# Graph layers on one Trainium2 core: one program per engine in place of four blocks, and rows dealt out 64 to a partition

## What is computed

```python
h = jnp.maximum(_layernorm(x, axis=-1), 0.0)
s = adj @ h[:, 0]
x = x + relu(h @ w_self.T + s[:, None] * jnp.sum(w_neigh, axis=1)[None, :])
h = jnp.maximum(_layernorm(x, axis=-1), 0.0)
Wh = (h @ W).reshape(n, 4, 64)                 # four heads
sl, sr = einsum(Wh, a_l), einsum(Wh, a_r)
e = leaky_relu(sl[:, :, None] + sr.T[None], 0.2)   # where adj + I > 0
x = x + elu(softmax(e) @ Wh)
```

## Time and profile before

| | us |
|---|---|
| median of three runs | 1027.2 |
| lowest, highest | 1024.8, 1027.9 |
| the profiled execution, its own time | 1026.3 |
| its span, first to last instruction | 1024.5 |
| PE busy | 701.5 (68%) |
| DVE busy | 709.2 (69%) |
| ACT busy | 337.7 (33%) |
| POOL busy | 397.3 (39%) |
| mean granted TensorE clock | 0.857 |
| read from HBM | 312.6 MB |

### The profile page before, as it was taken

One profiled execution on the slowest core, in us unless ns is written; L12 is line 12 of the kernel. 1 busy time (PEld: TensorE's weight loads), 2 busy tenths in 40 slices (PEclk: granted clock), 3 DMA queues, 4 the chain that ended last, 5 costly groups with the idle time before them and its releaser, 6 DMA issues. The chain is left out here.

```text
span 1024.5 us, 13553 instructions
## 1 busy us (share of the span) xinstructions
PE 701.5 (68%) x3025; PEld 464.3 (45%) x3026; DVE 709.2 (69%) x2868; ACT 337.7 (33%) x1481; POOL 397.3 (39%) x458
## 2 busy tenths in 40 slices
PE   1267866878677786768767787776527776777675
PEld 1034433544344443444444444544316665666564
DVE  5657676766766677766766667666237788778876
ACT  1023343343434334343433334334312222322222
POOL 0032323223232323223232232323077777777770
PEclk9978899888998889988898878887658889888878
DMA  9999999999999999999999999991034445545541
GB/s 299 414 422 419 422 422 422 423 425 422 423 420 425 419 418 422 421 405 396 421 422 409 401 415 405 411 407 62 27 106 119 133 128 144 140 133 132 139 127 49
DMA packets 70000, 321.94 MB, mean 314 GB/s; under 512 B 14498, under 2 KB 48721, under 8 KB 53536
## 3 DMA queue, kind: packets, MB, share of 16 engines
q1 hardware_dynamic: 44160, 293.88, 70.7%
q0 software_dynamic: 15360, 17.46, 7.4%
q10 hardware_dynamic: 10400, 9.74, 2.9%
HBM read 312.57 MB, written 17.07 MB: 322 GB/s over the span
## 5 line engine op out<-in xcount | busy, mean ns | idle before, releaser
L690 PE MATMUL p_pack<-big,pack_w 128*128 128x512 fp8e5 x1024 | 305.9, 450 | 165.6 <-DMA big<-in_adj_dram 148.8
L297 POOL DMA_INDIRECT h0g<-h_table,nbr x192 | 191.8, 999 | 473.3 <-ACT nbr L532 387.7
L690 PEld LDWEIGHTS p_pack<-big,pack_w 128*128 128x128 fp8e5 x1024 | 102.9, 106 | 313.7 <-issue 234.6
L917 POOL DMA_INDIRECT big<-row_table,lists x192 | 196.7, 1024 | 82.2 <-issue 56.7
L366 DVE MAX8 tops<-p_pack 128x8 f32<-128x256 f32 x128 | 48.9, 423 | 154.8 <-PE p_pack L690 154.8
L496 ACT ACTIVATE nbr<-keys 128x2 uint32<-128x2 f32 x64 | 13.0, 203 | 363.7 <-DVE keys L401 363.7
L957 PE MATMUL p_u<-big,ident 128*128 128x256 f32 x288 | 95.2, 480 | 51.6 <-DVE big L1086 51.6
L957 PEld LDWEIGHTS p_u<-big,ident 128*128 128x128 f32 x288 | 68.2, 245 | 67.2 <-DVE big L1086 54.8
L655 PE MATMUL p_u<-wselfT,hT 128*128 128x256 f32 x256 | 77.9, 434 | 0.0
L677 PE MATMUL p_row<-w_gat_and_heads,gT 128*128 128x264 f32 x256 | 69.8, 396 | 0.6 <-ACT rows L585 0.6
L1065 DVE TENSOR_TENSOR big<-big,p_pack 128x768 f32<-128x768 f32 x64 | 58.2, 949 | 1.1
(11 more groups left out here) (146 smaller groups left out, 1359.3 us busy)
## 6 DMA issues: line engine op xcount, KB each, us to landing
big<-in_adj_dram SPq DMA_DIRECT2D x128, 2048.0 KB, 18.3
row_table<-rows ACTq DMA_DIRECT2D x64, 132.0 KB, 9.5
big<-row_table SPq DMA_DIRECT2D x32, 264.0 KB, 3.1
x_rows<-in_x_dram SPq DMA_DIRECT2D x8, 1024.0 KB, 12.9
out_dram<-big SPq DMA_DIRECT2D x32, 256.0 KB, 3.1
h0g<-h_table,nbr POOLq DMA_INDIRECT x192, 6.2
big<-row_table,lists POOLq DMA_INDIRECT x192, 2.8
big<-in_L_gnn_w_self_dram ACTq DMA_DIRECT2D x1, 256.0 KB, 4.9
```

What stands on the lines that cost most here:

```text
L297: nc.gpsimd.indirect_dma_start(out=h0g[r][:, j:j + 1], out_offset=None, in_=h0_dram[:, :], in_offset=bass.IndirectOffsetOnAxis(ap=nbr[r][: ...
L690: last = nc.tensor.matmul(p_pack[:], pack_w[:, block_no, :], low_bytes(n % HALVES)[:, i, :], start=(block_no == 0), stop=(block_no == BLOC ...
L917: nc.gpsimd.indirect_dma_start(out=dst, out_offset=None, in_=row_dram[:, :], in_offset=bass.IndirectOffsetOnAxis(ap=lists[r][:, a, j:j + 1 ...
```

## The change

- The four blocks become one. Each engine gets one function that calls its parts of the four stages one after the other; only one barrier is left, at the end. What the barriers had ordered is now ordered by waits: ACT's wait for all row writes goes to SP and POOL, ahead of stage three (`all_rows_written`). SP and POOL also load the number of dense tiles there (`dense_rows_written`); POOL had not loaded it before.
- The two sums of flags move from stage two into PE's stage one (`sum_flags`, in the round of the last tile with lag 3, ahead of `first_product`).
- Row 64p+t is on partition p of tile t, where it was row 128t+p. So a piece of `x` is 8 KB of consecutive bytes on each partition, where it was eight rows of 1 KB, 128 KB apart. A load of adjacency is still 16 KB on each of 128 partitions, but from rows 2 MB apart. The own rows of a pair are 2112 consecutive bytes on a partition (were two pieces of 1056), the result of a pair 2 KB (were two of 1 KB). `row_table` and `h0_table` stay in order of row numbers.
- `h0c` is now written to `h0_table` as it lies: PE's turn and ACT's copy are gone.
- ACT's `sum_neighbours` is gone; DVE's first step of `update` adds the three values itself and waits for the gathers. POOL waits for that step in place of two others.

```diff
-    x_tiles = x.rearrange("(t p) d -> p t d", p=P)
+    x_tiles, out_tiles, row_tiles = (a.rearrange("(p t) d -> p t d", p=P) for a in (x, out, row_dram))
+    adj_tiles = adj.rearrange("(p t) m -> p t m", p=P)
...
-                        sp.dma_start(A[n % HALVES], adj[bass.ds(num(k, r) * P, P), s * HALF:(s + 1) * HALF]
+                    sp.dma_start(A[n % HALVES], adj_tiles[:, num(k, r), s * HALF:(s + 1) * HALF]
                                  ).then_inc(adj_in[n % HALVES], 16)
...
-                nc.gpsimd.iota(rown[:], [[P, TILES]], base=0, channel_multiplier=1,
+            nc.gpsimd.iota(rown[:], [[1, TILES]], base=0, channel_multiplier=TILES,
+            nc.gpsimd.iota(part_no[:], [[1, 1]], base=0, channel_multiplier=1,
...
                 if later_round(k):
-                        wait_alone(pool, s_summed, t - RING + 1)
-                        wait_alone(pool, u_ready, t - RING + 1)
+                    wait_alone(pool, upd_step, (t - RING) * UPD + 1)
...
                 wait_alone(dve, u_ready, t + 1)
-                    dve.wait_ge(s_summed, t + 1)
-                    step(nc.vector.tensor_tensor(stot[r][:], svec[r][:], p_first[:, D:D + 1], ALU.add), 1)
+                dve.wait_ge(h0_in[r], (k + 1) * 16 * OWN)
+                step(nc.vector.scalar_tensor_tensor(stot[r][:], h0g[r][:, 0:1], h0g[r][:, 1:2], p_first[:, D:D + 1],
+                                                    ALU.add, ALU.add), 1)
...
-                act.wait_ge(h0_turned, 1)
-                nc.scalar.copy(h0r[:], p_cnt[0:TILES, 0:P]).then_inc(h0_copied, 1)
-                act.wait_ge(h0_copied, 1)
-                act.dma_start(h0_dram.rearrange("(t p) o -> t (p o)", p=P), h0r[:]).then_inc(h0_out, 16)
+            act.wait_ge(h0_done, 1)
+            act.dma_start(h0_dram.rearrange("(p t) o -> p (t o)", p=P), h0c[:]).then_inc(h0_out, 16)
...
-                    act.dma_start(row_dram[bass.ds(t * P, P), :], rows[r][:]).then_inc(row_out[r], 16)
-                run(act, (sum_neighbours, 4), (list_neighbours, 1), (count_extras, 1), (keep_maps, 2), (pick_extras, 2),
+                act.dma_start(row_tiles[:, t, :], rows[r][:]).then_inc(row_out[r], 16)
+            run(act, (list_neighbours, 1), (count_extras, 1), (keep_maps, 2), (pick_extras, 2),
...
-                for r in range(RING):
-                    act.wait_ge(row_out[r], 16 * len(range(r, TILES, RING)))
...
+            def sum_flags(k, r):
+                if num(k, r) != TILES - 1:
+                    return
+                pe.wait_ge(flagged, TILES)
+                nc.tensor.matmul(p_cnt[:, 0:TILES], ones[:], flags_all[:], start=True, stop=True)
+                nc.tensor.matmul(p_cnt[:, TILES:2 * TILES], ones[:], extra_all[:], start=True, stop=True
+                                 ).then_inc(flags_summed, 1)
...
-                run(pe, (spread_extras, 2), (turn_first, 3), (first_product, 4), (turn_second, 5), (table_product, 6),
+            run(pe, (spread_extras, 2), (turn_first, 3), (sum_flags, 3), (first_product, 4), (turn_second, 5), (table_product, 6),
                         (pack_first, 0), (first_places, 1), (pack_second, 0))
...
+        def all_rows_written(eng):
+            for r in range(RING):
+                eng.wait_ge(row_out[r], 16 * len(range(r, TILES, RING)))
+        def dense_rows_written(eng):
+            eng.wait_ge(tiles_listed, 1)
+            with eng.If(eng.value_load(dense_count[0:1, 0:1], min_val=0, max_val=TILES) > 0):
+                eng.wait_ge(d_done, 1)
...
-                    sp.dma_start(G[r][:, :, 0, :], row_dram[bass.ds(t * (2 * P), 2 * P), :].rearrange("(a p) d -> p a d", p=P)
+                sp.dma_start(G[r][:, :, 0, :], row_tiles[:, two(k, r), :]
...
-                    sp.dma_start(out[bass.ds(t * (2 * P), 2 * P), :].rearrange("(a p) d -> p a d", p=P), res[r]
+                sp.dma_start(out_tiles[:, two(k, r), :], res[r]
...
+            @block.gpsimd
+            def _(pool):
+                gpsimd_fill_lists(pool)
+                gpsimd_attend_tiles(pool)
```

More of the change, by code:

```diff
@@ new lines, in sync_redo_dense_sums, with load @@
+        def sync_redo_dense_sums(sp):
+            def load(i, t):
+                all_rows_written(sp)
+                sp.wait_ge(d_free, i + 1)
+                sp.dma_start(x_at(t), of_tile(x_tiles, t)).then_inc(d_in, 16)
+                for s in range(2):
+                    sp.dma_start(A[s], of_tile(adj_tiles[:, :, s * HALF:(s + 1) * HALF], t)).then_inc(d_in, 16)
+                    sp.dma_start(h0_all[s], h0_dram[s * HALF:(s + 1) * HALF, :].rearrange("n o -> o n")
+                                 .broadcast_to([P, HALF])).then_inc(d_in, 16)
+            each_dense_tile(sp, load)
@@ new lines, in sync_attend_tiles, with own_rows, write @@
+        def sync_attend_tiles(sp):
+            def own_rows(k, r):
+                t = pair_no(k, r)
+                if later_pair(k):
+                    sp.wait_ge(mixed, t - RING2 + 1)
+                sp.dma_start(G[r][:, :, 0, :], row_tiles[:, two(k, r), :]
+                             ).then_inc(self_in[r], 16)
+            def write(k, r):
+                t = pair_no(k, r)
+                sp.wait_ge(res_ready, t + 1)
+                sp.dma_start(out_tiles[:, two(k, r), :], res[r]
+                             ).then_inc(pair_out[r], 16)
+            dense_rows_written(sp)
+            all_rows_written(sp)
+            run_pairs(sp, (own_rows, 0), (write, 5))
+            for r in range(RING2):
+                sp.wait_ge(pair_out[r], 16 * len(range(r, PAIRS, RING2)))
@@ new lines, in gpsimd_attend_tiles, with gather @@
+        def gpsimd_attend_tiles(pool):
+            def gather(k, r):
+                t = pair_no(k, r)
+                wait_alone(pool, lists_ready, t * 2 + 2)
+                if later_pair(k):
+                    wait_alone(pool, mixed, t - RING2 + 1)
+                for a in range(2):
+                    for j in range(OWN):
+                        dst = E[r][:, a, :] if j == DIRECT else G[r][:, a, j + 1, :]
+                        nc.gpsimd.indirect_dma_start(
+                            out=dst, out_offset=None, in_=row_dram[:, :],
+                            in_offset=bass.IndirectOffsetOnAxis(ap=lists[r][:, a, j:j + 1], axis=0),
+                            bounds_check=N - 1, oob_is_err=False).then_inc(rows_in[r], 16)
+            dense_rows_written(pool)
+            all_rows_written(pool)
+            run_pairs(pool, (gather, 0))
```

1448 lines of the change are left out of this document (703 added, 745 removed).

## The result

| | before | after |
|---|---|---|
| median of three runs | 1027.2 | 1064.9 |
| lowest, highest | 1024.8, 1027.9 | 1063.5, 1065.7 |
| the profiled execution, its own time | 1026.3 | 1063.5 |
| its span | 1024.5 | 1061.8 |
| mean granted TensorE clock | 0.857 | 0.851 |

The account below looks back on a forecast made before the run. Stage one was taken as bound by reading 268.4 MB, the second regime by POOL's gathers. Gains of 3.9 + 0.6 + 5.9 + 0.9 = 11.3 us took 1026.3 to 1015.0, with 0.9 for the median 1016; range 1010 to 1150, likeliest case 1010 to 1023.

Parts of the forecast that it names:

- The pitch: Rival, stage one's adjacency loads: rows 2 MB apart read slower, 129 us more, 1145 in all; chance 0.33.
- The start, 3.9: Loading x at the kernel's start: 8 KB pieces at the 16 KB rate save 3.9 us, ends 0 and 5.7.
- The steady state, 0: Changed steps per tile in stage one: all hidden by DMA, so 0 us.
- The drain, 0.6: Last rounds of stage one: update freed of ACT, less the sums of flags, gains 0.6 us; 1.3 lost to 1.3 gained.
- The passage, 5.9: From the last row writes to stage three's first gather: gather starts at 737.9, not 743.81, 5.9 us gained; 5.1 to 6.5.
- Stage three, 0: The same 192 gathers of the same rows; fewer pieces lie off the path, so 0 us.
- The end, 0.9: After the last result is written: one load and one barrier stay of two barriers and a load, 0.9 us gained.
- The sum, 11.3: Whole kernel: gains of 3.9, 0.6, 5.9 and 0.9 us make 11.3 us.
- The other rivals: Start and passage give nothing, 1024.3 us, chance 0.06; more tiles turn out dense, hundreds of us, under 0.01.
- Load 3: Adjacency load at stage one's start, released by weight preparation: forecast out at about 37, with 2 or 3 us to spare.

Follow-up runs that it names:

- chip B: One of five chips; the changed kernel took 1022.8 us there, the kernel before 1025.8.
- chip E: One of five chips; the changed kernel took 1022.6 us there, its twin with 4 KB of skew 1014.6, the kernel before 1024.5.
- runs of 8: Changed kernel with row 1024g+8p+j on partition p of tile 8g+j, adjacency rows 256 KB apart: 1015.1, 1016.6 and 1016.0 us on three chips.
- old rows: Changed kernel with rows dealt as before (row 128t+p on partition p) and the turn of h0c back: 1016.2 and 1017.4 us on two chips.
- chip A: One of five chips; the kernel before took 1026.1 us there, and its program with the new dealing of rows 1045.7.
- chip D: One of five chips, used for the terms of the gain; the kernel before took 1026.7 us there.
- chip C: One of five chips; the changed kernel took 1040.2 us there, the old program with new rows 1048.6, the kernel before 1027.5.
- the run with ACT's sum back: Rows in runs of 8, with the sum of the two direct values back on ACT: 1017.2 us, against 1016.0 without.
- the old program: Kernel before, four blocks and all waits kept, with only the new dealing of rows: 1045.7 us, 1.018 of before; 1048.6 on another chip.
- 2 MB less 32 KB: Changed kernel with 63 rows between neighbouring partitions' rows in an adjacency load, reading other windows of the matrix: 1013.8 us, 0.989 of before.

## Why the prediction was wrong, point by point

**The pitch: the step that failed.** The forecast took 421 GB/s unchanged as likeliest, "the one part that touches the bound itself", and gave the slower reading 0.33. The measured rate was 387 GB/s at full share. 268.4 MB at 387 take 694 us, 638 at 421: 56 by this, 51 by the last search, since the gap is narrower behind 400 us (390 against 411); 1016 + 51 = 1067 would have been the forecast, and 1064.9 was measured. The rival was the right mechanism at too low a chance, and its price, 129 us from the rate of `x` at 350 GB/s, was more than twice too high: 1 KB pieces were the wrong neighbour to take a size from. The argument against it, that engines up to 10 us apart aren't at the same place of their rows, fell: in the changed kernel one engine again works on alone, for some 9 us (share 0.07, about one of 16, from 742 to 748; the last pack starts at 751.24), and the loss is there all the same. On chips B and E the forecast's own 1016 was missed by only 6 to 7 us, so the sign rests on where it ran; that the pitch costs does not.

The Trainium skill, "DMA: Bandwidth & Descriptors", section "Latency and other measured facts", had it better than the forecast: for copies inside HBM it has a row pitch of 2 MiB well under the full rate, 512 KiB a little under it, and a pitch of 4 MiB at the full rate again once 4 KiB are added. The loads of this case agree on the first two (387 to 413 GB/s at 2 MB, 420 at 512 KB). They agree on the 4 KB as well, tried here at 2 MB and not at 4 (419 to 422). Its size at 2 MiB, 164 of 214 GB/s, came out smaller here: 387 of 421. It calls the aliasing of streams an inference, and that stays so: which part of the memory the streams meet in, no run shows.

**The start, 3.9.** Held at the start, not shown at the end. `x` came at 421 GB/s in 8 KB pieces, so the rate of the rows decided: 11 to 20% over that of the 1 KB pieces (349 to 379). The estimate of some 8% from the Trainium skill, "DMA: Bandwidth & Descriptors", section "Why small descriptors are slow", was too small. The timeline of the changed kernel, as in the earlier trace rows:

```profile
27.91 2.71 DVE L320 BATCH_NORM_STATS2 stat<-x_rows 128x6 f32<-128x256 f32 x8 [0.47 <-DMA x_rows<-in_x_dram]
...
32.14 1.28 ACT L480 ACT_TABLE_LOAD   x1
...
33.89 0.55 DVE L336 RECIPROCAL rstd<-tmp 128x64 f32<-128x64 f32 x1 [1.99 <-ACT tmp L480]
...
38.99 1.44 PE L668 MATMUL p_pack<-big,pack_w 128*128 128x512 fp8e5 x3 [7.28 <-DVE w_gat_and_heads L350]
```

The last statistics end at 30.6 ("by 31"), 5.2 us earlier, but the first pack starts only 3.8 earlier. ACT's table load stood at 19.3 in the kernel before; here it comes at 32.14, behind ACT's work on late weights (last section), and DVE waits 1.99 us for ACT where it waited 0.49. So the 3.8 is some 5.2 from `x`, more than was forecast, less 1.5 on ACT that the forecast had not seen; that it comes out at 3.9 is luck. Without the slow pitch the last search comes earlier: 704.5 with runs of 8 and 708.2 with old rows on chip A, 705.0 and 707.2 on chip D, so 3.7 and 2.2. The medians show only 1.1 and 1.4, and the first gathers 5.1 and 0.3; how much of the 3.9 reaches the end stays open.

**The steady state, 0.** Held within some 2 us: chip C has the two programs' last searches at 731.5 and 731.6.

**The drain, 0.6.** Under-sized, a little beyond its upper end of 1.3. It is 27.1 to 27.8 in profiles with ACT's sum, 23.8 to 27.5 without, the middle near 25.7: some 1.5. The forecast updates of tiles 62 and 63 at 723.25 and 726.0 came, on chip A with old rows, at 723.18 and 725.70:

```profile
721.55 0.33 PE L692 MATMUL p_cnt<-flags_all,ones 128*128 128x64 f32 x2
...
721.72 0.39 PE L693 MATMUL p_cnt<-extra_all,ones 128*128 128x64 f32 x2
...
723.18 0.21 DVE L459 SCALAR_TENSOR_TENSOR stot<-h0g,p_u 128x1 f32<-128x1 f32 x1 [1.44 <-PE p_u L653]
...
725.70 0.21 DVE L459 SCALAR_TENSOR_TENSOR stot<-h0g,p_u 128x1 f32<-128x1 f32 x1
```

The two sums of flags were priced at 1.1 us from a stretch at granted clock 0.50 (737 to 739). Here, at 0.82, they take PE from 721.55 to 722.11, 0.56 us. Moving them behind the products shortened one drain by 0.8, and ACT's sum put back lengthened one by 1.5; with the spread between drains neither is a proof.

**The passage, 5.9.** Held: 8.6 became 2.9 in every program without blocks that has the sum on DVE, 5.7 gained. The number was ready. What is waited for last came out the other way: SP, which waits for the row writes alone, issues its first load at 782.60; ACT's lists for the first pair are made at 782.82, and the first gather starts 0.91 behind them (0.84 before). The forecast had the lists 0.3 ahead of the landing, and they were some 0.2 behind it. The run with ACT's sum back agrees: its passage is 2.6, and its first gather again starts 0.92 behind the lists.

**Stage three, 0.** 252.2 us from first to last gather and not 253.9, but 254.4 in the new program with old rows: the spread of single profiles, not a gain.

**The end, 0.9.** Held. SP leaves its last wait for results 2.2 us before the end of the span in the kernel before and 1.2 in the changed one, 1.1 or 1.2 in the others. (The 0.9 of the table above is no proof, by the spread given there.)

```profile
L905 SPq EVENT_SEMAPHORE  x2: 17/22/28, 1020.6 to 1022.3; - x2
```

```profile
L887 SPq EVENT_SEMAPHORE  x1: 28/28/28, 1060.6 to 1060.6; - x1
```

**The sum, 11.3.** Runs of 8, which have all the parts of the change but the pitch, gained 11.0, 10.9 and 10.7 us on chips A, C and D. The program alone, 7.4 by the terms, gained 9.9 and 9.3 by the medians on old rows, and 8.4 on new ones (chip C: 1048.6 - 1040.2), so 1 to 2.5 us more than its terms; 0.9 of that is the drain's. Dealing the rows in runs of 8 added 1.1 and 1.4 to it where 3.9 were forecast. That the sum comes out within half a microsecond of 11.3 is therefore in part luck: one part gave more and the other less, each by about as much as two medians tell.

**The other rivals** did not come up. Load 3 went out at 38.99 (37 forecast) and from 38 to 48 us the DMA share is 1.01, so it was in time; no tile was dense, or the second half would have been longer by hundreds of us.

## What to carry to other kernels

Before dealing rows out another way, work out the distance between partitions in each large load: at 2 MB between 128 streams the read fell by 2 to 8% at full DMA share, at 1 MB a little, at 512 KB and below by nothing that could be told, and 4 KB more or one row less undid it. A run of 8 rows to a partition has all that the long run was to bring (8 KB pieces, one piece a pair) at 256 KB. And where a change touches the resource that bounds the kernel, ask first about that part: eleven microseconds elsewhere paid for the mild losses here (8 to 9 us, the kernel then 2 or 3 us faster than before) and not for the others (23 and 51).

## What the runs showed of the hardware that was not expected

- The loss from one and the same pitch differs between occasions: 51 us at first, then 26 (chip A, in the old program: last search 730.7, against 704.5 with runs of 8), 23 (chip C), 9 (chip E) and 8 to 9 (chip B, against 2 MB less 32 KB), with the kernels beside it alike. A verdict on such a layout from one chip says little about the next.
- One of the 16 DMA engines ends its part of the 268 MB some 9 us behind the others, with either layout (and share 0.07 from 742 to 748 after).
- A load in 1 KB pieces that shares the engines with 8 KB pieces waits longer. The weights on ACT's queue, before and after, by their DMA issue:

```profile
big<-in_L_gnn_a_r_dram ACTq DMA_DIRECT2D x1, 128.0 KB, 10.8
```

```profile
big<-in_L_gnn_a_r_dram ACTq DMA_DIRECT2D x1, 128.0 KB, 23.9
```

It landed at 27 us. The preparation of weights on PE and ACT began only then and ran into ACT's part of the statistics, which cost the start 1.5 us. Runs of 8 have the same (23.8 us to landing, DVE waits 2.16).
